# Adapter attention: alternate masked and adapter pairs, lag the second pass 26 steps, spread the background

## What is computed

```python
q, k, v = heads(x @ Wq), heads(x @ Wk), heads(x @ Wv)      # 32 heads of 8
q, k = rope(q), rope(k)
w = softmax(q @ k.T / sqrt(8) + mask)                      # masked scores
out = w @ v
a_k, a_v = heads(ctx @ Wk), heads(ctx @ Wv)                # adapter, no rope, no mask
out = out + (tanh(gate) * softmax(q @ a_k.T / sqrt(8))) @ a_v
x = layernorm(x + merge(out) @ Wo)
```

## Time and profile before

| what | us |
|---|---|
| median of three runs | 1207.67 |
| span of the profiled execution | 1209.3 |
| TensorE busy (by modelled ends) | 1141.4 (94%) |
| VectorE busy | 991.1 (82%) |
| ScalarE busy | 658.8 (54%) |
| GpSimd busy | 655.4 (54%) |

### The profile page before, as it was taken

One profiled execution on the slowest core, in us unless ns is written; L12 is line 12 of the kernel. 1 busy time (PEld: TensorE's weight loads), 2 busy tenths in 40 slices (PEclk: granted clock), 3 DMA queues, 4 the chain that ended last, 5 costly groups with the idle time before them and its releaser, 6 DMA issues.

```text
span 1209.3 us, 29549 instructions
## 1 busy us (share of the span) xinstructions
PE 1141.4 (94%) x11172; PEld 935.9 (77%) x11172; DVE 991.1 (82%) x2282; ACT 658.8 (54%) x1687; POOL 655.4 (54%) x706
## 2 busy tenths in 40 slices
PE   5899999899999999879999999999999999999998
PEld 5677676666666766546799899998999999988886
DVE  6668787788889888977888888988898888867877
ACT  5465554566666667564555444444444444556663
POOL 4456656435455455253778554444544455746665
PEclk9899999999999999988999999999999999998999
DMA  5875442343333333301212000000000100101111
GB/s 155 206 180 135 124 128 81 86 105 104 93 100 103 97 103 92 113 19 51 83 61 71 1 1 2 1 1 2 1 1 1 36 2 1 36 4 35 36 36 36
DMA packets 98558, 76.22 MB, mean 63 GB/s; under 512 B 73547, under 2 KB 86987, under 8 KB 98417
## 3 DMA queue, kind: packets, MB, share of 16 engines
q1 hardware_dynamic: 98417, 74.34, 22.9%
HBM read 53.40 MB, written 19.92 MB: 61 GB/s over the span
## 4 chain that ended last, share of the span: by engine, by line
PE 65%; DVE 19%; issue 6%; ACT 5%; POOL 2%; DMA 1%; SPq 1%; POOLq 0%; DVEq 0%; ACTq 0%
PE bank L1517 5%; PE bank L1518 4%; PE bank L1519 4%; PE bank L1573 4%; PE bank L1546 4%; PE bank L611 4%; DVE B_nr L737 4%; DVE PT L746 3%; PE bank L547 3%; PE bank L554 2%; PE bank L472 2%; PE bank L589 2%; PE bank L1533 2%; PE bank L1588 2%; PE bank L1586 2%
## 5 line engine op out<-in xcount | busy, mean ns | idle before, releaser
L1821 POOL TENSOR_TENSOR C_QK<-C_t1b,C_t2b 128x512 f32<-128x512 f32 x128 | 168.9, 1320 | 228.6 <-DVE C_t2b L1660 228.1
L1657 DVE SCALAR_TENSOR_TENSOR C_t1b<-bank,C_bcol,C_tabs 64x512 f32<-64x512 f32 x256 | 192.0, 750 | 39.3 <-PE bank L1519 35.3
L737 DVE TENSOR_REDUCE B_nr<-bank 128x4 f32<-128x512 f32 x256 | 164.4, 684 | 26.2 <-PE bank L554 25.0
L985 ACT ACTIVATE PT<-bank 128x512 f32<-128x512 f32 x160 | 92.0, 597 | 50.2 <-PE bank L589 49.9
L1517 PE MATMUL bank<-C_XTh,C_Wh 128*128 128x512 f32 x256 | 112.9, 441 | 4.4 <-DVE C_XTl L1506 1.9
L1753 ACT ACTIVATE C_P<-bank,C_nm 128x128 f32<-128x128 f32 x256 | 90.7, 367 | 34.1 <-DVE C_nm L1670 32.4
L978 ACT ACTIVATE PT<-PT 128x512 f32<-128x512 f32 x96 | 59.4, 630 | 91.1 <-DVE PT L746 91.1
L1772 ACT ACTIVATE C_V<-bank 128x512 f32<-128x512 f32 x64 | 38.1, 597 | 124.1 <-PE bank L1535 122.5
L1518 PE MATMUL bank<-C_XTl,C_Wh 128*128 128x512 f32 x256 | 101.9, 398 | 0.0
L1519 PE MATMUL bank<-C_XTh,C_Wl 128*128 128x512 f32 x256 | 101.5, 396 | 0.0
L611 PE MATMUL bank<-PT,vpool 128*32 128x128 f32 x2048 | 97.8, 286 | 3.9 <-ACT PT L978 3.8
(11 more groups left out here) (266 smaller groups left out, 3669.9 us busy)
## 6 DMA issues: line engine op xcount, KB each, us to landing
Adrq<-PB SPq DMA_DIRECT2D x16, 192.0 KB, 3.5
Adrk<-PB SPq DMA_DIRECT2D x16, 192.0 KB, 3.1
stk<-Adrq SPq DMA_DIRECT2D x16, 192.0 KB
stk<-Adrk SPq DMA_DIRECT2D x16, 192.0 KB
Bdrq<-PB SPq DMA_DIRECT2D x16, 192.0 KB, 2.8
stk<-Bdrq SPq DMA_DIRECT2D x32, 96.0 KB
Bdrk<-PB SPq DMA_DIRECT2D x16, 192.0 KB, 2.7
stk<-Bdrk SPq DMA_DIRECT2D x32, 96.0 KB
```

The lines of the kernel that those rows point to most:

```text
L737: e.tensor_reduce(dst, bank[n % 2][:, :].rearrange("p (a b) -> p a b", a=4), AX.X, ALU.max, negate=True).then_inc(sem("m_dve"), 1)
L1657: e.scalar_tensor_tensor(out=v4(t1b[kq][lo:lo + 64, :]), in0=v4(o[hi:hi + 64, :]), scalar=bc[hi:hi + 64, :], in1=tabsC[hi:hi + 64, 2 * kq ...
L1821: e.tensor_tensor(QK[v % 3][:, kq, :], t1b[kq][:, :], t2b[kq][:, :], ALU.add).then_inc(sem("rc_pool"), 1)
```

## The change

- Layer B's units: pairs alternate now between masked (kd 0) and adapter (kd 1) within a batch: i, kd and t follow from the unit's number. The last masked unit of a batch is its 14th, the last adapter unit its 16th. The semaphore counts that follow from the order (`last_unit`, `v_masked`) and the waits in `pass1` are adapted: the wait for the keys' stack stands before a batch's first pair, that for the adapter stack before its second.
- pass2 lags 26 steps instead of 28 (LAG), and LAST_FIRST is 294.
- Background of chunks 10 to 15: transposes at -4 and 10 (were -8 and 8), projections at -1, 7, 13 (were -5, 10, 13), the mask's turn at 23 (18), the values at 19, 25, 17, 35 (7, 23, 26, 30), in another order.
- The outputs: the masked part ends two steps before the adapter part, both are turned one step after their end, the turn back comes 4 steps ahead of the output projection (3), the shift rows are turned 2 steps after their step (4).
- On GpSimd shift_parts of layer B stands before the splits and the rope of its step, not behind them.

```diff
-    LAST_FIRST = 292
+    LAG = 26
+    LAST_FIRST = NN - LAG
...
-        kd, r = divmod(r, 2 * NI[L])
         if not L:
             t, i = divmod(r, NI[L])
-            return L, b, kd, t, i, [4 * (n % 4) + j for j in range(4)]
-        i, t = divmod(r, 2)
+            return L, b, 0, t, i, [4 * (n % 4) + j for j in range(4)]
+        i, kd, t = r // 4, r // 2 % 2, r % 2
...
-        return 4 * g + 3 if g < 16 else NA + 16 * (g - 16) + 8 * kd + 7
+        return 4 * g + 3 if g < 16 else NA + 16 * (g - 16) + 13 + 2 * kd
...
-        return 8 * (u // 16) + u % 16 + 1
+        return 8 * (u // 16) + u % 16 // 4 * 2 + u % 2 + 1
...
-        return [s - 12] if 12 <= s < NA + 12 else pair(s - 28)
+        return [s - 12] if 12 <= s < NA + 12 else pair(s - LAG)
...
-    STEPS = NN + 28 + 2 + 12
+    STEPS = NN + LAG + 2 + 12
...
-    xts = places((-1,), (-2, -4), (-2, 2), (-8, 8))
-    projs = places((2, 6), (2, 6, 10), (0, 8, 13), (-5, 10, 13))
-    masked = places((), (12,), (21,), (18,))
+    xts = places((-1,), (-2, -4), (-2, 2), (-4, 10))
+    projs = places((2, 6), (2, 6, 10), (0, 8, 13), (-1, 7, 13))
+    masked = places((), (12,), (21,), (23,))
     clamps = {s - (3 if c < 10 else 7): c for s, (c, _) in masked.items()}
-    vals = places((3, 5), (4, 15, 8, 16), (19, 22, 20, 24), (7, 23, 26, 30))
+    vals = places((3, 5), (4, 15, 8, 16), (19, 22, 20, 24), (19, 25, 17, 35))
...
-        return 4 * g + 18 if g < 16 else NA + 16 * (g - 16) + 8 * kd + 37
+        return 4 * g + 18 if g < 16 else NA + 16 * (g - 16) + 2 * kd + LAG + 15
...
-        return end_step(g, kd) + (7 if 16 <= g < 31 and kd else 1)
+        return end_step(g, kd) + 1
...
-    backs = {wo_step(g) - (2 if g == 14 else 3 if g == 15 else 3 if 16 <= g < 31 else 2): g for g in range(32)}
+    backs = {wo_step(g) - (2 if g == 14 else 3 if g == 15 else 4 if 16 <= g < 31 else 2): g for g in range(32)}
...
-    turned = {shift_step(g) + (2 if g < 16 else 4 if g < 31 else 2): g for g in range(32)}
+    turned = {shift_step(g) + 2: g for g in range(32)}
...
-                if n % U[L] == 0 or (L and n % 8 == 0):
-                    q.wait_ge(*stack_sem(L, b, "a" if kd else "k"))
+                if n % U[L] == 0:
+                    q.wait_ge(*stack_sem(L, b, "k"))
+                if L and n % U[L] == 2:
+                    q.wait_ge(*stack_sem(L, b, "a"))
...
+            if s in shifts and shifts[s] >= 16:
+                shift_parts(e, q, shifts[s], "sh_pool")
             for part in range(2):
                 if s in splits[part] and splits[part][s] not in FIRST:
                     split(e, q, *splits[part][s], part)
...
-            if s in shifts and shifts[s] >= 16:
-                shift_parts(e, q, shifts[s], "sh_pool")
```

More of the change, by code:

```diff
@@ L174, in k_val @@
     def k_val(c, n, b):
-        return 2 * c + b if c < 8 else 16 + 4 * (c - 8) + ((0, 2, 1, 3) if c < 10 else (0, 1, 2, 3))[2 * n + b]
+        return 2 * c + b if c < 8 else 16 + 4 * (c - 8) + ((0, 2, 1, 3) if c < 10 else (1, 2, 0, 3))[2 * n + b]
     def v_masked(n):
         u = n - NA
-        return 8 * (u // 16) + u % 16 + 1
+        return 8 * (u // 16) + u % 16 // 4 * 2 + u % 2 + 1
     def stack_left(i, k):
```

## The result

The changed kernel takes **1260.89 us** (1259.76 to 1266.08), the kernel before 1209.47 on the same chip: ratio **1.0428 [1.0405, 1.0451]**. The forecast was 1228, with a range of 1200 to 1242: the sign was right, the size less than half (+20.6 forecast, +51.4 measured). Spans of the profiled executions: 1258.4 against 1209.3 us, +49.1.

What follows compares the result with a forecast made beforehand. TensorE and VectorE were both taken as near their limit in layer B. Six chunks at +2.8 (+16.8), the start +4.5, the third batch +1.4 and the lag -2.1 gave +20.6 us, so 1228, range 1200 to 1242.

Steps and rivals of the forecast that it cites:

- What bounds the kernel: Layer B: TensorE and VectorE both near their limit; reordering can win only idle time, 5.6 us a chunk on VectorE.
- Part 1: Layer B's alternating masked and adapter pairs: VectorE idles in masked slots, +2.5 us a chunk (bounds -1.5 and +4).
- Part 2: Layer B's adapter stack wanted sooner: TensorE waits 0.1 to 1.4 us a chunk, taken as 0.3.
- Last two batches: End of layer B: no loss forecast, as only the six chunks between steps 96 and 288 were counted.
- Start: Start of layer B: TensorE held 4.5 us for the adapter stack; clock fall up to 5 more, chance 0.15.
- Third batch: Layer B's third batch: adapter stack landed 233.8, wanted 232.40, so +1.4 us.
- Part 3: Shorter lag at layer B's end: one slot fewer without a first pass, -2.1 us (0 to -3).
- Part 4: Layer B's background spread to one product a slot: same products, no separate cost, counted in Part 1.
- the third, SP's queue as the bound: Rival: adapter stack costs 1.4 us in every chunk instead of 0.3; 1235, or 1240 with slower landing; chance 0.2.
- The first, balance: Rival: layer B's engine peaks fall in different slots, VectorE's 3.6 us idle a chunk goes; 1195, chance 0.27.

Runs made afterwards that it cites:

- x2: Changed kernel with only SP's stack transfers reordered (odd batch's query stack behind the adapter stack; first chunk's odd keys later): 1242.53 us, ratio 1.0253.
- x9: x2 with the old order of units (eight masked, eight adapter) in all sixteen batches: 1251.94 us, ratio 1.0346.
- x11: Kernel before with the new background places, earlier shift, its parts ahead of the splits on GpSimd, and x2's stack order: 1224.59 us, ratio 1.0119.
- x13: x2 with lag 30 instead of 26, the mask and one masked value product 4 steps later: 1246.09 us, ratio 1.0295.
- x10: Kernel before with lag 26, the shift turned two steps earlier and its parts ahead of the splits on GpSimd: 1259.74 us, ratio 1.0417.
- x8: x2 with the old order of units in batches 0, 14 and 15 of layer B: 1231.11 us, ratio 1.0172.
- x4: Kernel before with only the background's new places and the new order of the values: 1240.08 us, ratio 1.0248.
- x15: x2 with all steps of stage C's preparation two lower: 1233.05 us, ratio 1.0173.
- x12: Kernel before with only the shift turned two steps earlier and its parts ahead of the splits on GpSimd: 1209.82 us, ratio 0.9991.
- x14: Changed kernel with the old background places, except the mask's: 1269.96 us, ratio 1.0481.
- x7: Kernel before with only lag 26: 1253.06 us, ratio 1.0342.
- x17: x15 with batch 0 of layer B in the old order of units: 1226.22 us, ratio 1.0131.

## Why the prediction was right on the sign and had less than half the size

- **What bounds the kernel**: VectorE's busy time did not change, and the chunk grew by its idle time, as I had it.
- **Part 1, +2.5 a chunk**: right in size, not in what makes it. x2, free of late stacks, has +2.1 in S3 to S6 and +3.2 in S7. By rows: OTl 2.2 for 2.0, residual 0.8 for 1.4, x_low 0.8 for 0.8, division nothing for 0.4, OS gone. But it is the price against the kernel before, for the whole change at once, and I put it to the alternation. x9 shows that the alternation gains 12.4 over these stretches on top of lag and background, and that the waits at OTl (1.7) and at the residual (0.8) are there without it; x11 pays 2.0 a chunk with the background alone. So the agreement of 2.5 with 2.1 is in part luck. The mechanism as I wrote it, masked and adapter slots in turn make the loss, is not shown, and x9 speaks against it.
- **Part 2, adapter stack 0.3 a chunk**: the step that failed. In S3 to S7 the changed kernel and x2 differ by 3.9, 2.0, 4.8, 1.8 and 2.6, 3.0 in the mean, ten times what I took and twice my upper bound. The queue's sum was right: from the start of the shift rows to the last issue of the adapter stack I had 407.2-389.6=17.6, and it took 17.4 (317.60 to 334.99) and 17.6 (416.52 to 434.14) in the chunks with no long group, 18.9 in the case shown. What I had wrong is when TensorE wants the stack. I had it 19.7 after the start of the shift rows, 4.0 more than the 15.7 of the kernel before (408.02-392.3): a slot of 2.76 for the earlier shift and 1.25 for longer slots. It was 18.0 to 18.2, in x2 as well: at most 2.5 more. For S4 that gives 17.4, 2.5 to the landing and less 18.0, a wait of 1.9 (1.92 measured), for S6 17.6+2.35-18.2=1.75, and up to 3.20 where an issue or a landing took longer. A second part came on top, which I had priced for the start alone: S3 and S5 have a clock of 0.97, and lost some 1.5 each by it. The stretches grew by 48.8 us against the 20.6 of the forecast; of the 28 between, 13.6 are this term in S3 to S7 and 5.6 the same in S8.
- **Last two batches, 0**: failed. S8 grew by 9.3: 5.6 were the same late stack (TensorE waited 3.84 at 534.09) and its clock of 0.85. I had ended the count of chunks at step 288, though batch 14 reads a stack as well. x2 still has a part of both there, a wait of 1.42 and a clock of 0.96. But x13 has neither, and its S8 is 40.7; so some 3.4 are open. S8 is 37.5 in x11 (lag 28, new background), 39.1 in x10 (lag 26, old background), 41.8 in x8 and 42.8 in x9, which have both.
- **Start, +4.5 and the clock**: the hold was 5.7 us at 188.67, of the kind that I described, and the fall of the clock, given 0.15, came: 0.81 while TensorE was idle, then 0.50 from 188.6 to 192 and 0.79 to 196. A score group took 0.61 us there and 0.40 at full rate. S1 grew by 8.0. Over it, 2 x (1-0.91) x 59.7 = 10.7 us were at half rate, none before. Some 2 of the 8.0 are not the hold: x4 and x11, with the new background and no wait for a stack, have an S1 of 53.8 and 53.5 against 51.6. The Trainium skill, TensorE: Matmul & The Clock Gate, Part 1, says that an idle TensorE is gated to half rate until it is busy again. The trace agrees at this hold, where the clock was at 0.50 when TensorE began again; it does not fall after every wait, though (S7: 2.52 us of wait, clock 1.00). My reading that the trace before has the fall after such gaps only was too strong: its clock is at 0.50 from 1104 to 1110 us as well, and the longest wait of TensorE in the ten microseconds ahead of that is 0.86.
- **Third batch, +1.4, with 2.8 for its chunk**: no wait for a stack and +1.1 in S2. Too high.
- **Part 3, lag -2.1**: failed, +3.7 (of which up to 3 can be the spread between executions). The steps of stage C are fixed numbers and did not move with the lag; moved by two they give 7.5 us (x15), and the rest is then 3.5 shorter than before. A fixed step beside a moving end was the term that I had put at nothing. That the early parts on GpSimd cost nothing was right (x12).
- **Part 4, background at no cost of its own**: right only inside this change, where the old places would cost 9 us more (x14). Its places and the lag belong together: alone they cost 29 (x4) and 42 us (x7).
- **Rivals**: the third, SP's queue as the bound, had the right mechanism and too low a price, 1235 to 1240 with a chance of 0.2. The first, balance, has a real gain in it, 9 us, against a base that is 41 us worse. No version beat the kernel before; the best with the alternation, x17, is 1.3% behind.

## What to carry to other kernels

In a kernel whose work is placed by hand in steps, edits are not additive: moving one stream by two steps may bring three products into one slot, and only the tables together say so. So list, for each stream that moves, what stands at its new step, and which fixed step numbers hang on an end that moves. For a queue with a deadline, sum the issues, and work out the deadline with the same care: read in the old trace how long after the queue's first entry its result is wanted, and let a wait of a microsecond or two stand as a wait, for the clock behind it can cost as much again.

## What the runs showed of the hardware

- Six stack transfers took SP 3.74 to 4.98 us to issue in one and the same kernel, 0.62 to 0.83 each; the landing was 2.0 us after the last had been issued in the case shown. The issues followed each other without a pause (368.64+4.98=373.62, the next at 373.67) in chunks whose DMA share is 0.32 to 0.35: the issue time, not the bytes, filled the queue.
- Short holds can take the clock with them. Before, S1 to S8 had a clock of 1.00 throughout; in the changed kernel S1 had 0.91, S3 and S5 0.97, S8 0.85. In S3 the wait of 2.33 us ended at 287.77, and the clock of 289 to 293 was 0.57. S3 and S5 are 1.9 and 3.0 us longer than S4 and S6, whose clock is 1.00; their waits for the stack (2.33 and 3.20 against 1.92 and 1.75) explain 0.4 and 1.4 of it, which leaves some 1.5 each for the slower clock. That fits the clock: 2 x (1-0.97) x 50 = 3 us at half rate lose 1.5.
- The length of a wait alone does not say whether the clock falls. In S7 TensorE waited 2.52 us, longer than in S3, and the clock stayed at 1.00.
